# Node rows of a graph layer made by GpSimd, and one routing step moved in front of the first expert

## The chip, the core and the metric

One core of a Trainium2 chip runs the whole kernel. The metric is the device time of one execution, in microseconds (us), and the median of several executions is compared. The core has five engines with queues of their own: TensorE (PE; its weight loads are PEld), VectorE (DVE), ScalarE (ACT), GpSimd (POOL) and SyncE (SP, which here only issues DMAs).

## The reference

A graph attention layer is followed by a mixture of experts. There are 3750 nodes of 256 features, 120,000 edges sorted by destination and 8 relations with 4 heads:

```
h = segment_sum(ex * feat_src) / segment_sum(ex)       # per destination node and head
x = x + h + bias                                       # the "node rows"
xn = layernorm(x);  logits = xn @ Wr + br
two best of 8 experts per node; weights from the softmax of their two logits
x = x + sum over the two experts of  w_e * (gelu(layernorm(xn) * g_e + b_e) @ W1_e + b1_e) @ W2_e + b2_e)
```

## The kernel before

The nodes lie in 30 tiles of 128 rows. Three stages follow each other, and each is a block that all engines enter and leave together.

**Node stage.** It computes the features of each node for each relation and stores them in DRAM. Its GpSimd adds the bias to x (L392).

**Edge stage** (`edge_stage`). It runs over 32 groups of edge blocks. GpSimd gathers features (L798). VectorE scales them (L905) and adds sums from PSUM into `acc` (L914). TensorE multiplies by one-hot matrices (L1154). `acc` holds, per node, 256 weighted sums and 4 denominators. The last group is written out by hand in `last_period` of the vector block. There the first tile of the group is first rescaled (`carry_over`, L919 and L921), and then the sums are added pair by pair. Four PSUM banks hold the sums, so the matmul of a pair waits until VectorE has added the pair four before it. GpSimd has issued its last gather at 1806.6 us and then idles to the end of the stage.

**Route and expert stage** (`route_expert_stage`). It works in three batches of node tiles, 0 to 5, 6 to 15 and 16 to 29 (`BATCHES_R`). Most work goes by pairs of tiles. For a batch:

- `inverse` makes 1/denominator (L1768, L1769).
- `mean_pair` multiplies `acc` by it (L1750), and `node_pair` adds the mean to the node rows `xs` (L1754). `xs` lies in a buffer of `gath` and was loaded near the end of the edge stage. In batch 2 ScalarE makes the means (L1686) and VectorE only the sums.
- TensorE turns each pair (L1524) and multiplies by the router's weights (`pair_logits`, L1538); ScalarE copies the turned pair between the two (L1656).
- `statistics` (L1774) and `moments` (L166 to L171, L1782, L1783) make mean and variance. ScalarE takes the root (`deviation`, L1652). `factors` (L1789, L1790) makes scale and offset, and ScalarE writes the normalised rows (L1663).
- `choose` (L1799 to L1816) finds the two best experts. `counts` on TensorE (L1545 to L1547) counts rows per expert. `weigh` on ScalarE makes the weights (L1670). `place` (L1824 to L1840) turns all this into slots.
- GpSimd scatters each tile twice into `slots_x` in DRAM (L1482), in the order of the tiles.
- `hand_out` gives the expert steps their expert and their first row. Then `table_ready` lets SP load weights and rows.

An expert step n is `turn(n)` (L1556), `affine(n)` on VectorE (L1888), `first_layer(n)` (L1571), `gelu(n)` on ScalarE (L1680), `second_layer(n)` (L1587), `results(n)` on VectorE (L1901, L1904) and `add(n)`, an indirect DMA by GpSimd that adds to `out` (L1496). There are 43 steps. The order of all this on each engine is written out by hand. SP loads rows 0 and 1 when batch 0 is scattered. `ADDS_AFTER` says behind which tile's scatter GpSimd issues an `add`. The row loads from step 5 on wait for the scatters of batch 1.

The order in question on VectorE is: inverse, nodes, statistics and moments of batch 0, choose(0), inverse of all other tiles, place(0), nodes(1), hand_out, statistics and moments of batch 1, the node sums of batch 2, five of its statistics, then keep_tail(0), affine(0), choose(1), keep_tail(1), affine(1), place(1).

Of the kernel before, what the change touches and what calls it, by code (L numbers as in the profile page):

```python
# [24 lines left out]
ALU = mybir.AluOpType  # L25
# [3 lines left out]
P = 128  # L29
N_NODES = 3750  # L30
N_EDGES = 120000
D = 256
HEADS = 4
# [591 lines left out]
def edge_stage(nc, sb, edges, feats, xb, wr, br):  # L625
# [6 lines left out]
    with ExitStack() as ctx:  # L632
# [133 lines left out]
        with nc.Block() as block:  # L766
# [19 lines left out]
            @block.gpsimd  # L786
            def _(pool):
                def gather_features(g, r, n):
                    if not there(g):
                        return  # L790
                    if not isinstance(g, int) or g >= AHEAD:
                        wait_apart(pool, idx_ready, g - (AHEAD - 1), carrier)
                    for j in range(quads(g)):
                        if not isinstance(g, int) or g >= GBUFS:

                            wait_apart(pool, sum_ready, freed(g, j), carrier)
                        for u in range(j * QUAD, (j + 1) * QUAD):
                            pool.indirect_dma_start(gath[:, r, u], None, feats,  # L798
                                                    bass.IndirectOffsetOnAxis(ap=idxT[:, r, u:u + 1], axis=0)).then_inc(gath_in[r], 16)

                each_period(pool, gather_features, GBUFS + 1, GROUPS - 2)

            @block.vector
            def _(dve):
# [131 lines left out]
                def last_period(g, r, ra):  # L936
# [16 lines left out]
                    add(a, 7, ra, sums7)  # L953
                    carry_over(g, sums0[0])
# [285 lines left out]

def step_index(n):

    if n < FIRST3:
        return n
    at = HALVES_OF[FIRST3:n].count(HALVES_OF[n])
    return FIRST3 + (at if HALVES_OF[n] == 2 else N_BIG + at)

def route_expert_stage(nc, sb, experts1, experts2, b2, slots_x, out):
# [6 lines left out]
    with ExitStack() as ctx:  # L1256
# [18 lines left out]
        rden = t("rden", [P, TILES, HEADS])  # L1275
# [111 lines left out]

        def batch_of(n):
            return [n < hi for _, hi in BATCHES_R].index(True)
# [12 lines left out]
        with nc.Block() as block:  # L1402
            @block.sync
            def _(sp):
# [19 lines left out]
                def store(b):  # L1424
                    sp.wait_ge(xs_ready, BATCHES_R[b][1] // 2)
                    sp.dma_start(out_tiles[:, batch(b)], xs[:, batch(b)]).then_inc(out_stored[b], 16)
# [10 lines left out]
                sp.wait_ge(xs_ready, BATCHES_R[1][1] // 2)  # L1437
# [35 lines left out]
            def _(pool):  # L1473
# [31 lines left out]
                ADDS_AFTER = {10: [0], 13: [1], 15: [2], 18: [3], 22: [4]}  # L1505
# [10 lines left out]
            def _(pe):  # L1516
                def turn_pair(p):
                    pe.wait_ge(xs_ready, p + 1)
# [97 lines left out]
                turn_pair(first)  # L1616
                turn(0)
                first_layer(0)
                turn(1)
                counts(1)  # L1620
# [27 lines left out]
            def _(act):  # L1648
# [66 lines left out]
                copy_pair(first)  # L1715
                gelu(0)
                weigh(1)
# [22 lines left out]
            def _(dve):  # L1740
# [15 lines left out]
                def nodes(b):  # L1756

                    lo, hi = BATCHES_R[b][0] // 2, BATCHES_R[b][1] // 2
                    dve.wait_ge(x_in[b], 16)
                    mean_pair(lo)  # L1760
                    for p in range(lo, hi):
                        if p + 1 < hi:
                            mean_pair(p + 1)
                        dve.wait_ge(mean_done, p + 1)
                        node_pair(p)

# [4 lines left out]
                def statistics(b, of):  # L1771
                    dve.wait_ge(xs_ready, BATCHES_R[b][1] // 2)
# [134 lines left out]
                inverse(batch(0))  # L1907
                nodes(0)
# [67 lines left out]
def build(nc, ins, out):  # L1976
# [3 lines left out]
    with ExitStack() as ctx:  # L1980
# [22 lines left out]
        sb["small_in"] = ctx.enter_context(nc.semaphore("small_in"))  # L2003
        sb["x_in"] = [ctx.enter_context(nc.semaphore(f"x_in_r{b}")) for b in range(len(BATCHES_R))]
# [50 lines left out]
```

## Time and profile before

| | |
|---|---|
| median of 3 runs | 2462.4 us (2460.36 to 2465.61) |
| span of the profiled execution (first to last instruction) | 2456.4 us |
| mean granted TensorE clock | 0.813 |
| edge stage ends, route stage starts | 1883.4 us |
| first expert's first matmul | 1931.3 us |
| PE busy in 2100 to 2456 us | 345.2 of 356 us |
| weights of one expert step (w1, w2, b2), by the DMA issues | 1030 + 1024 + 128 KB |

The profile has no time for its execution beside the span; the median of the runs is 6.0 us above it, which is what lies before the first and behind the last instruction. A span is read stage by stage: TensorE is busy 77% of it as a whole, and nearly all of the last part.

### The profile page before, as it was taken

What the parts mean: (1) busy time and instruction counts of PE and PEld (TensorE: products, weight loads), DVE (VectorE), ACT (ScalarE), POOL (GpSimd) and SP (SyncE); (2) the same over time, 40 slices, a digit from 0 to 9 for tenths busy, and PEclk for the clock granted to TensorE, in tenths of its full rate; (3) what the DMA queues carried; (4) which work ended last, traced back from release to release, by engine and by line L of the source; (5) the groups of instructions that cost most, each with busy time, mean ns of one, the idle gap of its engine ahead of it and who ended that gap; (6) DMA issues with size and microseconds to landing.
All of it is one profiled execution on the core that took longest, in us unless ns stands there. A gap on an engine that the chain in (4) does not pass through costs nothing. (4 is left out here: it accounts for less than half of the span.)

```text
span 2456.4 us, 35279 instructions
## 1 busy us (share of the span) xinstructions
PE 1898.8 (77%) x9138; PEld 1594.8 (65%) x9139; DVE 1062.3 (43%) x3018; ACT 1076.9 (44%) x3259; POOL 1142.0 (46%) x1164
## 2 busy tenths in 40 slices
PE   8999125767767777867777777677877689999998
PEld 7887124656655665656565666565665668999887
DVE  6332013545555555545555555455567532221111
ACT  2222123645555545554555555454656532222221
POOL 4000744556666566666666566656620443122222
PEclk9999556787877768777787777777788689999999
DMA  6443422333333333333333333333312877777774
GB/s 239 189 170 143 109 67 74 84 90 88 90 92 92 88 88 91 90 88 90 88 92 92 89 90 90 92 85 88 91 44 80 282 230 221 248 246 247 241 234 104
DMA packets 121157, 315.51 MB, mean 128 GB/s; under 512 B 27047, under 2 KB 71335, under 8 KB 106180
## 3 DMA queue, kind: packets, MB, share of 16 engines
q0 software_dynamic: 60192, 149.24, 23.4%
q1 hardware_dynamic: 60836, 164.88, 19.3%
q8 instruction: 41, 0.67, 0.1%
q14 instruction: 88, 0.72, 0.1%
HBM read 257.36 MB, written 57.71 MB: 128 GB/s over the span
## 5 line engine op out<-in xcount | busy, mean ns | idle before, releaser
L798 POOL DMA_INDIRECT gath<-feats,idxT x996 | 950.6, 954 | 799.1 <-issue 272.7
L1154 PE MATMUL psP<-gath,hot 128*128 128x260 f32 x1992 | 668.1, 493 | 28.6 <-DVE gath L905 15.1
L1154 PEld LDWEIGHTS psP<-gath,hot 128*128 128x128 f32 x1992 | 469.4, 247 | 123.5 <-issue 35.4
L1113 PE MATMUL psOT<-cst,hot 128*128 128x128 f32 x996 | 196.1, 331 | 346.0 <-ACT hotT L1045 231.9
L1045 ACT COPY hotT<-psOT 128x512 f32<-128x512 f32 x249 | 143.5, 576 | 628.6 <-remote 485.4
L1113 PEld LDWEIGHTS psOT<-cst,hot 128*128 128x128 f32 x996 | 139.7, 171 | 407.2 <-issue 309.0
L1138 PEld LDWEIGHTS psE<-er,hotT 128*128 128x128 f32 x1992 | 309.7, 235 | 48.6 <-issue 44.9
L914 DVE TENSOR_TENSOR acc<-acc,psP 128x260 f32 x498 | 211.0, 424 | 295.3 <-remote 127.9
L1138 PE MATMUL psE<-er,hotT 128*128 x1992 | 309.5, 305 | 31.1 <-issue 19.9
L1035 ACT ACTIVATE hot<-cst,ndlT 128x128 f32<-128x128 f32 x996 | 316.2, 391 | 4.7 <-PEq L325 4.7
L1680 ACT ACTIVATE acc<-psH,w1buf 128x256 f32<-128x256 f32 (+1 forms) x344 | 122.4, 423 | 346.7 <-PE psH L1571 304.3
L1063 ACT ACTIVATE gath<-gath 128x64 f32<-128x64 f32 x1040 | 261.0, 337 | 0.1
L1496 POOL DMA_INDIRECT out<-acc,node x66 | 103.3, 1565 | 335.0 <-DVE acc L1904 178.0
L1571 PE MATMUL psH<-acc,w1buf 128*128 128x256 f32 (+1 forms) x1376 | 241.9, 334 | 4.4 <-issue 2.4
L1587 PE MATMUL psY<-w2buf,acc 128*128 128x256 f32 x1056 | 240.9, 384 | 3.4 <-issue 3.3
L905 DVE TENSOR_TENSOR gath<-gath,psA 128x1024 f32<-128x1024 f32 x184 | 224.5, 1221 | 27.2 <-ACT gath L1075 19.9
L1571 PEld LDWEIGHTS psH<-acc,w1buf 128*128 128x128 f32 x1376 | 217.8, 194 | 24.8 <-DVE acc L1888 2.9
L585 PE MATMUL psF<-wext,xT 128*128 128x264 f32 x960 | 221.1, 388 | 1.1 <-ACT xT L536 1.1
L1587 PEld LDWEIGHTS psY<-w2buf,acc 128*128 128x128 f32 x1056 | 200.0, 193 | 32.4 <-issue 6.8
L585 PEld LDWEIGHTS psF<-wext,xT 128*128 128x128 f32 x960 | 180.7, 191 | 31.6 <-ACT xT L536 1.5
L1038 ACT ACTIVATE hot<-hot 128x512 f32<-128x512 f32 x249 | 156.8, 630 | 38.3 <-remote 25.9
L1888 DVE TENSOR_SCALAR acc<-psX,w1buf 128x256 f32<-128x256 f32 (+1 forms) x86 | 37.5, 478 | 214.8 <-PE psX L1556 186.1
(232 smaller groups left out, 1178.5 us busy)
## 6 DMA issues: line engine op xcount, KB each, us to landing
w1buf<-in_experts SPq DMA_DIRECT2D x43, 1030.0 KB
w2buf<-in_experts SPq DMA_DIRECT2D x43, 1024.0 KB
feats<-frow SPq DMA_DIRECT2D x29, 1040.0 KB, 3.9
gath<-feats,idxT POOLq DMA_INDIRECT x996
meta<-in_edges SPq DMA_DIRECT2D x464, 12.0 KB
acc<-slots_x SPq DMA_DIRECT2D x23, 258.0 KB
gath<-in_b SPq DMA_DIRECT2D x43, 128.0 KB
acc<-slots_x SPq DMA_DIRECT2D x20, 129.0 KB
```

The costliest lines, as they stand in the source:

```text
L585: ins = pe.matmul(psF[:, n % BUFS, j, 0:W], xT[:, i % LEAD, k], wext[:, k, 2 * pair + j], start=k == 0, stop=k == KD - 1)
L798: pool.indirect_dma_start(gath[:, r, u], None, feats, bass.IndirectOffsetOnAxis(ap=idxT[:, r, u:u + 1], axis=0)).then_inc(gath_in[r], 16)
L905: dve.tensor_tensor(feat, feat, alpha.unsqueeze(3).to_broadcast([P, QUAD, HEADS, HD]), ALU.mult).then_inc(scaled, 1)
L914: dve.tensor_tensor(into[b % PQ], into[b % PQ], psP[:, bank(g, b, r), 0:FW], ALU.add).then_inc(sum_used, 1)
L1035: ins = act.activation(hot[:, r, u], iota, ACT.Square, bias=ndlT[:, r, u:u + 1])
L1038: act.activation(hot[:, r, j * QUAD:(j + 1) * QUAD], hot[:, r, j * QUAD:(j + 1) * QUAD], ACT.Relu, bias=1.0, scale=-1.0).then_inc(hot_read ...
L1063: ins = act.activation(feat, feat, ACT.Copy, scale=gath[:, r, u, D + h:D + h + 1])
L1113: ins = pe.transpose(psOT[:, k * P:(k + 1) * P], hot[:, r, j * QUAD + k], ident)
L1138: ins = pe.matmul(psE[:, u * W % 512:u * W % 512 + W], hotT[:, j % 2, k * P:(k + 1) * P], tables[k // BLK], start=True, stop=True)
L1154: ins = pe.matmul(psP[:, bank(g, b, r), 0:FW], hot[:, r, u], gath[:, r, u], start=u % BLK == 0, stop=u % BLK == BLK - 1)
L1571: ins = pe.matmul(psH[:, bank(n, g), at * slots(n):(at + 1) * slots(n)], w1(n, k, m), xeT[:, n % 2, k, 0:slots(n)], start=k == 0, stop=k = ...
L1587: ins = pe.matmul(psY[:, y_bank(n, j), 0:D], hT[:, n % 2, m, j * P:(j + 1) * P], w2(n, m), start=m == 0, stop=m == KH - 1)
```

## The change

GpSimd makes the means and node rows of pairs 0 to 6 (tiles 0 to 13), pairs 0 to 2 still inside the edge stage and pairs 3 to 6 in the route stage. For this VectorE makes 1/denominator of tiles 0 to 15 inside `last_period`, between the last add of the group before and `carry_over`. VectorE keeps pair 7. A pair is two GpSimd instructions of 128 x 512 f32, a product and a sum, both read twice from SBUF.

In the route stage choose(1) and place(1) of VectorE go in front of keep_tail(0) and affine(0), counts(1) of TensorE in front of turn(0), and weigh(1) of ScalarE in front of gelu(0). GpSimd scatters batch 1 up to tile 13 without a break, and then does add(0), where it did add(0) behind tile 10. The adds 1, 2 and 3 go behind tile 15.

```diff
@@ edge stage, GpSimd
                 each_period(pool, gather_features, GBUFS + 1, GROUPS - 2)
+                pool.wait_ge(sb["rden_early"], 1)
+                nodes_by_pool(pool, sb, 0, BATCHES_R[0][1] // 2, sb["x_in"][0])
@@ edge stage, last_period of VectorE
                     add(a, 7, ra, sums7)
+                    early = slice(0, BATCHES_R[1][1])
+                    step(dve.tensor_scalar(sb["rden"][:, early], acc[:, early, D:FW], 1e-30, None, ALU.max))
+                    step(dve.reciprocal(sb["rden"][:, early], sb["rden"][:, early]))
+                    dve.sem_inc(sb["rden_early"], 1)
                     carry_over(g, sums0[0])
+def nodes_by_pool(pool, sb, lo, hi, x_in):
+    def mean_pair(p):
+        t = slice(2 * p, 2 * p + 2)
+        part = acc[:, t, 0:D].rearrange("p t (h d) -> p t h d", h=HEADS)
+        pool.tensor_tensor(part, part, rden[:, t].unsqueeze(3).to_broadcast([P, 2, HEADS, HD]), ALU.mult).then_inc(mean_pool, 1)
+    mean_pair(lo)
+    pool.wait_ge(x_in, 16)
+    for p in range(lo, hi):
+        t = slice(2 * p, 2 * p + 2)
+        if p + 1 < hi:
+            mean_pair(p + 1)
+        pool.wait_ge(mean_pool, p + 1)
+        pool.tensor_tensor(xs[:, t], xs[:, t], acc[:, t, 0:D], ALU.add).then_inc(xs_pool, 1)
@@ route stage, GpSimd
                 ins.then_inc(keep_ready, 1)
-                ADDS_AFTER = {10: [0], 13: [1], 15: [2], 18: [3], 22: [4]}
+                nodes_by_pool(pool, sb, BATCHES_R[1][0] // 2, BY_POOL, x_in[1])      # BY_POOL = 7
+                ADDS_AFTER = {13: [0], 15: [1, 2, 3], 22: [4]}
@@ route stage, TensorE
                 turn_pair(first)
+                counts(1)
                 turn(0)
                 first_layer(0)
                 turn(1)
-                counts(1)
@@ route stage, ScalarE
                 copy_pair(first)
+                weigh(1)
                 gelu(0)
-                weigh(1)
@@ route stage, VectorE
-                inverse(batch(0))
-                nodes(0)
                 dve.wait_ge(sums_ready, 1)
...
                 factors(0)
+                mean_pair(BY_POOL)
+                dve.wait_ge(x_in[1], 16)
+                dve.wait_ge(mean_done, 1)
+                node_pair(BY_POOL)
                 dve.wait_ge(keep_ready, 1)
                 choose(0)
-                inverse(slice(BATCHES_R[0][1], TILES))
+                inverse(slice(BATCHES_R[1][1], TILES))
                 dve.sem_inc(rden_ready, 1)
                 place(0)
-                nodes(1)
                 units_left()
...
                 statistics(2, range(0, 5))
+                choose(1)
+                place(1)
                 keep_tail(0)
                 affine(0)
-                choose(1)
                 keep_tail(1)
                 affine(1)
-                place(1)
```

Whoever waited for `xs_ready` (the transposes, the statistics, SP's stores) now waits for GpSimd's count `xs_pool` up to pair 6 and for VectorE's from pair 7 (`wait_nodes`, `wait_batch`).

## Rows read from the trace of the kernel before

**Rows 1.** The page: busy time by engine; chain that ended last, by engine.
```profile
PE 1898.8 (77%) x9138; PEld 1594.8 (65%) x9139; DVE 1062.3 (43%) x3018; ACT 1076.9 (44%) x3259; POOL 1142.0 (46%) x1164
PE 20%; issue 1%; DMA 1%; POOL 0%; DVE 0%; another core or an unknown queue 0%; ACT 0%; SPq 0%; DVEq 0%; POOLq 0%
```

**Rows 2.** Windows: length, busy us by engine (instructions), granted clock, DMA share, GB/s.
```profile
1900.00:1920.00 20.00, 11.47 (x52) 10.58 (x52) 18.52 (x58) 16.57 (x61) 13.53 (x12) 0.50 0.50 170
1920.00:1940.00 20.00, 11.99 (x73) 11.11 (x73) 9.83 (x40) 11.25 (x23) 0.00 (x0) 0.63 1.03 362
1940.00:1960.00 20.00, 13.63 (x85) 12.92 (x84) 9.81 (x46) 7.37 (x17) 13.36 (x14) 0.80 0.72 251
...
2100.00:2456.00 356.00, 345.20 (x1845) 309.52 (x1843) 68.53 (x218) 86.64 (x240) 77.97 (x50) 0.99 0.71 219
```

**Rows 3.** Chain of waits, 1880 to 1960 us: start, length, what.
```profile
1883.67 0.31 DVE rden L1769
...
1916.77 6.56 DMA slots_x<-gath,slot_i
...
1924.12 5.58 DMA acc<-slots_x
...
1931.26 5.58 PE psH L1571 x32
...
1944.49 10.01 another core or an unknown queue
```

**Rows 4.** Timeline of VectorE and TensorE, end of the edge stage: start, length, instruction.
```profile
1875.09 0.43 DVE L921 TENSOR_TENSOR acc<-acc,phi 128x256 f32 x1
1875.55 0.99 DVE L914 TENSOR_TENSOR acc<-acc,psP 128x260 f32 x2
...
1872.82 9.20 PE L1154 MATMUL psP<-gath,hot 128*128 128x260 f32 x40 [0.89 <-DVE gath L905]
```

**Rows 5.** Timeline of GpSimd and VectorE, node stage.
```profile
0.26 0.10 POOL L2048 MEMSET const-float32-1.0<- 128x1 f32 x1
32.37 2.78 POOL L392 TENSOR_TENSOR x_biased<-x_rows,bias_all 128x256 f32<-128x256 f32 x4 [25.05 <-DMA bias_all<-in_bias]
...
32.43 0.71 DVE L167 TENSOR_TENSOR std<-stats 128x10 f32<-128x10 f32 x1
...
34.53 0.65 DVE L170 TENSOR_TENSOR mean<-stats 128x10 f32<-128x10 f32 x1
```

**Rows 6.** Timeline of VectorE, start of the route stage.
```profile
1887.94 2.06 DVE L1774 BATCH_NORM_STATS2 stats_r<-gath 128x6 f32<-128x256 f32 x6
1890.03 0.17 DVE L166 TENSOR_TENSOR mean_r<-stats_r 128x6 f32<-128x6 f32 x1
...
1894.14 0.21 DVE L1799 TENSOR_TENSOR lg<-psY,scl 128x48 f32<-128x48 f32 x1 [1.54 <-PE psY L1538]
...
1898.30 0.75 DVE L1769 RECIPROCAL rden<-rden 128x96 f32<-128x96 f32 x1
...
1900.15 0.17 DVE L1836 CAST slot_i<-slot_f 128x12 int32<-128x12 f32 x1
...
1910.47 0.16 DVE L1873 TENSOR_SCALAR row_of<-row_f 1x5 int32<-1x5 f32 x1
```

**Rows 7.** Timeline of ScalarE, route stage.
```profile
1899.14 6.79 ACT L1686 ACTIVATE acc<-acc,rden 128x64 f32<-128x64 f32 x28 [0.65 <-DVEq L1926]
...
1915.84 0.22 ACT L1652 ACTIVATE std_r<-std_r 128x20 f32<-128x20 f32 x1
```

**Rows 8.** Timeline of GpSimd and TensorE, route stage.
```profile
1951.60 0.97 POOL L1482 DMA_INDIRECT slots_x<-gath,slot_i  x1 [0.30 <-issue]
1948.69 0.39 PE L1571 MATMUL psH<-acc,w1buf 128*128 128x128 f32 x2 [0.55 <-issue]
...
1955.16 1.88 PE L1538 MATMUL psY<-wr_even,xtT 128*128 128x8 f32 x8 [4.80 <-ACT xtT L1656]
...
1989.70 7.17 PE L1571 MATMUL psH<-acc,w1buf 128*128 128x256 f32 x32 [0.89 <-DVE acc L1888]
```

More of the change, by code:

```diff
@@ L953, in last_period @@
                     add(a, 7, ra, sums7)
+                    early = slice(0, BATCHES_R[1][1])
+                    assert BASES[LAST] - (EBLOCKS - 1) >= BATCHES_R[1][1]
+                    step(dve.tensor_scalar(sb["rden"][:, early], acc[:, early, D:FW], 1e-30, None, ALU.max))
+                    step(dve.reciprocal(sb["rden"][:, early], sb["rden"][:, early]))
+                    dve.sem_inc(sb["rden_early"], 1)
                     carry_over(g, sums0[0])
@@ L1238, in rows_of_nodes @@
     return words[:, 0:TILES * D].rearrange("p (t d) -> p t d", t=TILES)
+def nodes_by_pool(pool, sb, lo, hi, x_in):
+    acc, rden, xs, mean_pool, xs_pool = sb["acc"], sb["rden"], rows_of_nodes(sb), sb["mean_pool"], sb["xs_pool"]
+    def mean_pair(p):
[10 more added lines that the diff above has]
+        pool.tensor_tensor(xs[:, t], xs[:, t], acc[:, t, 0:D], ALU.add).then_inc(xs_pool, 1)
 def step_index(n):
@@ L1274, in route_expert_stage @@
         wr_even = t("wr_even", [P, KD, E])
-        rden = t("rden", [P, TILES, HEADS])
+        rden, xs_pool = sb["rden"], sb["xs_pool"]
         stats = t("stats_r", [P, BT, 6])
@@ L1386, in pair_bank, with wait_nodes, wait_batch @@
             return p % 2 if p < BATCHES_R[2][0] // 2 else 1
+        BY_POOL = BATCHES_R[1][1] // 2 - 1
+        def wait_nodes(eng, p):
+            if p < BY_POOL:
+                eng.wait_ge(xs_pool, p + 1)
+            else:
+                eng.wait_ge(xs_ready, p - BY_POOL + 1)
+        def wait_batch(eng, b):
+            hi = BATCHES_R[b][1] // 2
+            wait_nodes(eng, min(hi, BY_POOL) - 1)
+            if hi > BY_POOL:
+                wait_nodes(eng, hi - 1)
         def batch_of(n):
@@ L1424, in store @@
                 def store(b):
-                    sp.wait_ge(xs_ready, BATCHES_R[b][1] // 2)
+                    wait_batch(sp, b)
                     sp.dma_start(out_tiles[:, batch(b)], xs[:, batch(b)]).then_inc(out_stored[b], 16)
@@ L1436, in _ @@
                 load_weights(1)
-                sp.wait_ge(xs_ready, BATCHES_R[1][1] // 2)
+                wait_batch(sp, 1)
                 sp.wait_ge(scattered[0], 32 * SIZE[0])
@@ L1517, in turn_pair @@
                 def turn_pair(p):
-                    pe.wait_ge(xs_ready, p + 1)
+                    wait_nodes(pe, p)
                     free = p - 1 if p < BATCHES_R[2][0] // 2 else p
@@ L1754, in node_pair @@
                     dve.tensor_tensor(xs[:, t], xs[:, t], acc[:, t, 0:D], ALU.add).then_inc(xs_ready, 1)
[L1756 to L1765, printed above, removed]
                 def inverse(of):
@@ L1771, in statistics @@
                 def statistics(b, of):
-                    dve.wait_ge(xs_ready, BATCHES_R[b][1] // 2)
+                    wait_batch(dve, b)
                     for i in of:
@@ L2003, in build @@
         sb["small_in"] = ctx.enter_context(nc.semaphore("small_in"))
+        sb["rden"] = keep("rden", [P, TILES, HEADS])
+        sb["rden_early"], sb["xs_pool"] = ctx.enter_context(nc.semaphore("rden_early")), ctx.enter_context(nc.semaphore("xs_pool"))
+        sb["mean_pool"] = ctx.enter_context(nc.semaphore("mean_pool"))
         sb["x_in"] = [ctx.enter_context(nc.semaphore(f"x_in_r{b}")) for b in range(len(BATCHES_R))]
```

## The prediction

> **What bounds the kernel now.** I read the page first. TensorE is busy 77% of the span and no other engine reaches half; the chain that ended last is named TensorE for a fifth of the span and hardly anything else [rows 1]. The windows by stage say where that holds. In 2100 to 2456 us TensorE is busy 345 of 356 us at full clock, and a change here could not shorten it. In 1900 to 1940 us it is busy 23.5 of 40 us at a clock of 0.50 and 0.63 [rows 2]. So what the change can win or lose is the time at which the packed expert part begins, plus gaps up to about 1990 us. The third view, the chain of waits, gives the order of that stretch: inverse, nodes and statistics of batch 0 on VectorE, logits, choose(0), place(0), then 12 scatters, 6.56 us until the last has landed, 5.58 us to load rows 0, and first_layer(0) at 1931.26 [rows 3]. Slots of batch 0 are ready at 1900.3 [rows 6], call it S; first_layer(0) starts at S + 30.9.
>
> **What an instruction of GpSimd costs.** The trace has a sum of 128x256 with both inputs in SBUF: 4 in 2.78 us, 0.70 each. A memset of one element is 0.10 [rows 5]. For 128x512 the bounds are 0.70 (no price per element) and 1.40 (twice). With 0.1 fixed it is 1.3 and I take that. No row shows a product with a broadcast input; I give it the same.
>
> **What it does to VectorE.** Before the first of those four GpSimd instructions VectorE's small sums take 0.17 us [the same kind in rows 6]. While the four run, its instructions L167 to L170, also with two inputs in SBUF, take 0.71 to 0.65 us each [rows 5]: one goes through per GpSimd instruction and GpSimd is not slowed. So beside instructions of 1.3 us I price each such VectorE instruction at 1.3. The lower bound is its own length, 0.17.
> The Trainium skill (SBUF — State Buffer, Who interferes with whom) says this of the chip: a VectorE instruction with two SBUF inputs contends with a GpSimd instruction that reads SBUF, and the later one blocks until the other is done. The trace agrees, 0.71 instead of 0.17 us. By that rule work handed to GpSimd isn't beside VectorE's but in its way; without the rule the sum would be the first rival below.
>
> **Part 1, end of the edge stage.** Added to VectorE are one small scalar instruction (0.2) and a reciprocal of 64 columns; between 0.31 for 24 and 0.75 for 96 columns it is 0.55 [rows 3, 6]. With the waits that is 0.8 us in front of carry_over. GpSimd then starts its first product, and L921 (acc times phi, both in SBUF, normally at 1875.09) waits for its end, at 1875.7 + 1.3 = 1877.0. The adds of the group start at 1877.6, not 1875.55 [rows 4]. TensorE's 40 records take 9.2 us, 0.92 a pair; it runs two quads by 1876.5 and then needs the first pair added. From there VectorE's order (two adds, a scale, two adds, 1.0 + 1.2 + 1.0 us) paces it: pair 9 ends 6.5 us behind the first add, at 1884.1 instead of 1882.0. The stage ends 2.1 us later, at 1885.5. Bounds: 0.85 if L921 isn't held, 3.3 if L919 in front of it is held too. GpSimd's six instructions, 7.8 us and the 0.45 of L921, end at 1884.0 and are hidden; at 1.4 each they still are.
>
> **Part 2, to the slots of batch 0.** Times from the stage's start (T). VectorE loses inverse and nodes of batch 0, 0.5 + 3.6 us. It waits for the ones' product (0.95) and makes its six statistics (2.06) by 3.2; before it was 6.6. GpSimd starts its eight instructions at 0.6 and ends at 11.0. Moments has five instructions with two SBUF inputs (1.0 us before), each now one GpSimd instruction long: it ends at 10.5, not 4.9. Before it ended at 8.0. Constants and factors, 1.15, are done at 11.65; pair 7 on VectorE, 0.69 twice and a wait, at 13.1. The logits are no longer what choose(0) waits for: TensorE can turn pairs from 0.9 and needs about 7.6 us (1886.0 to 1894.0 before), 8.5. choose(0) 3.8, inverse of 14 tiles 0.8, place(0) 1.15 [rows 6]: slots at T + 18.9 = 1904.4, against 1900.3. S moves by +4.1.
>
> **Part 3, from the slots to first_layer(0).** nodes(1), 6 us, is gone between place(0) and hand_out, so the table is ready at S + 4.2 instead of S + 10.3 [rows 6], and SP's first two sets of weights, 4.4 MB, go out 6 us sooner. They no longer share the DMA (half busy in 1900 to 1920, full behind it [rows 2]) with the last scatters and with rows 0: 3 us less for each of the two [rows 3]. So rows 0 land at about S + 24 instead of S + 29.4. They are no longer last. ScalarE's 14 means and four copies take 15.4 us from rden_ready and end the root of batch 1 at R + 16.7 [rows 7], R being S - 1.2: S + 15.7 with its latency. VectorE must wait for it in factors(1) (0.5), then has four node sums (2.5) and five statistics (1.7), then choose(1), which had run behind affine(0) (17 instructions as in choose(0), each some 0.03 longer for 80 columns: 4.4): S + 24.9. TensorE's counts(1) is 0.9, turn(0) ends at S + 26.5. ScalarE's ten normalised tiles and one copy end at 24.7, a table load (1.28) and weigh(1) at 26.3. place(1) 1.1, keep_tail and affine(0) 1.0: first_layer(0) at S + 28.7. Against S + 30.9 that is -2.2. With S at +4.1 the first layer starts 1.9 us later, 1933.1.
>
> **Part 4, behind it.** Before, GpSimd issues ten scatters of batch 1, 0.97 and 0.30 each, the last at 1951.60, so from 1940.1 to 1952.6; then it waits for add(0). In this stretch ScalarE stands for 10 us, with a releaser that the profile doesn't know, until 1954.5 [rows 3], and TensorE, busy 13.6 of 20 us, goes on at 1955.16 [rows 2, 8], 2.6 us behind the last scatter. What holds it I can't tell; the run of scatters is the nearest thing in time. Now place(1) ends at S + 27.4, 16 scatters of 1.27 us start 0.9 behind it at 1932.7 and end at 1953.0. If the stall goes with their end, TensorE continues at 1955.6, +0.4 us. The lower bound is no stall, the upper one with more of TensorE's work behind it, both below. Scattering tiles 14 and 15 sooner takes away the late load of step 5, and with it 0.9 us of gap at 1989.7 [rows 8]. The moved adds cost nothing: GpSimd's share is 1.6 us each and results(2) needs add(0) only near 1980.
>
> **Sum.** +1.9 at the first layer, -1.5 until 1955, -0.9 at step 5: -0.5 us on a span of 2456.4. The runs' median is 6.0 above the span, so I predict 2462 us. A difference under 0.2%, 4.9 us, can't be told from none.
>
> **Rivals.**
> 1. *No interference, or a short GpSimd instruction.* L921 isn't held (stage end +0.85), moments ends at T + 4.9, pair 7 is done at 7.5 and the logits at 8.5 set choose(0): slots at T + 14.2 = 1898.5, S at -1.8, the first layer at -4.0, and with the -2.3 of part 4 the sum is -6.3: 2456. For it: nodes really leave VectorE, 10 us in all. Against: rows 5.
> 2. *The stall of 1944 to 1955 goes.* Weights are in earlier, DMA has less piled up. TensorE would not stand 6 us, nor run at half clock until about 1964 (4 us): 2452 to 2454. For it: a DMA share of 1.03 in 1920 to 1940. Against: it is 0.72 in 1940 to 1960, not full, and the stall is there [rows 2].
> 3. *The longer run of scatters starves the others* (slower). 16 instead of 10 without a break, starting with first_layer(0) and not 9 us into the experts. TensorE's matmuls break up at 1948.1, 8 us into the run of before [rows 8]. At 1932.7 + 8 = 1940.7 it would have done 7.4 us less of its work than at 1948.1 before, and resume at the same 1955.6: +7 us, 2469. It decides if any engine's supply ends within the first 12 us of the run. Against: beside the 12 scatters from 1901 on ScalarE makes its means without a gap [rows 7].
> 4. *The change does its part but L919 is held too and moments' scalar instructions as well*: +1.2 and +1.0 more, 2464; inside "same".
>
> **Chances.** Forecast, with rival 4, 0.42; rival 1 0.21; rival 2 0.16; rival 3 0.21. Faster by over 0.2%: most of rivals 1 and 2, and the forecast's lower tail, 0.36. Slower: rival 3 and an upper tail of 0.04, 0.25. Same 0.39. The forecast's own range is 2458 to 2466. To hold 8 in 10 it must reach rival 2 below and rival 3 above: 2451 to 2470.
>
> **What would show it.** GpSimd's 128x512 at 1.3 us; VectorE's L166 to L170 at 1.3 us each beside them, L921 held; the route stage starting near 1885.5; slots of batch 0 near 1904; the table 4 us behind them; factors(1) waiting for ScalarE; first_layer(0) near 1933; TensorE standing until some 2.6 us behind the sixteenth scatter; no gap in front of step 5. I am wrong if L166 to L170 stay at 0.17 us, or if the gaps of 1940 to 1960 change by more than 3 us.

## The result and the profile after

The kernel after takes 2470.2 us in the median of 14 runs, the kernel before 2460.5 in 14 runs of the same chip: ratio 1.0038, 95% interval [1.0026, 1.0051]. On a second chip, with 5 runs of the kernel after, it was 1.0063 [1.0045, 1.0080]. So the change costs 0.4 to 0.6%, 10 to 15 us, where I forecast no difference; the time lies 0.2 us above the upper end of my range (2470).

The page after, busy time by engine and the chain by engine. It answers to [rows 1], and looks the same: the loss is not to be seen there.
```profile
PE 1888.1 (76%) x9138; PEld 1585.3 (64%) x9139; DVE 1059.5 (43%) x3004; ACT 1077.4 (44%) x3260; POOL 1155.3 (47%) x1178
PE 20%; DVE 1%; issue 1%; ACT 1%; another core or an unknown queue 0%; POOL 0%; DVEq 0%; POOLq 0%
```
The windows after (columns as in [rows 2]; the last is moved by 10 us).
```profile
1900.00:1920.00 20.00, 7.63 (x36) 7.13 (x36) 17.02 (x74) 16.50 (x51) 8.09 (x9) 0.50 0.21 58
1920.00:1940.00 20.00, 9.29 (x42) 8.39 (x42) 9.33 (x26) 14.42 (x33) 5.43 (x6) 0.50 0.86 312
1940.00:1960.00 20.00, 12.72 (x78) 11.44 (x78) 8.55 (x37) 5.30 (x12) 11.63 (x12) 0.77 0.95 310
1960.00:1980.00 20.00, 14.69 (x70) 12.96 (x70) 5.67 (x30) 7.15 (x17) 8.12 (x8) 0.66 0.42 147
...
2110.00:2466.00 356.00, 348.98 (x1874) 313.15 (x1872) 69.75 (x220) 88.91 (x248) 79.10 (x51) 0.99 0.73 222
```
From 1900 to 1960 TensorE is busy 29.6 us, 7.5 less than the 37.1 of [rows 2]; from 2110 on it is as full as before. So the loss arises ahead of the packed experts, where I had looked for any change. The profiled spans differ by 13.6 us (2470.0 and 2456.4), the medians by 9.7. The profiled run after took 1.8 us more than its span, and all other runs that have both figures on record 1.8 to 1.9; the 6.0 us that I added to the span of before is thus for the most part a profiled execution that was faster than the median. By marks in the two timelines (one profiled run each) the 13.6 us are:

| stretch | before | after | difference |
|---|---|---|---|
| VectorE's last sum of the edge stage ends | 1882.9 | 1886.9 | +4.0, of which 2.35 were there ahead of the first changed instruction |
| from there to the route stage's start (T) | 0.5 | 5.4 | +4.9 |
| T to the slots of batch 0 (S) | 16.9 | 18.7 | +1.8 |
| S to first_layer(0) | 30.9 | 34.1 | +3.1 |
| first_layer(0) to step 5 (first 128x256 layer) | 58.4 | 60.1 | +1.7 |
| step 5 to the end | 466.7 | 464.8 | -1.9 |

**The start of the route stage.** VectorE and GpSimd at the end of the edge stage after (start, length, instruction; it answers to [rows 4]).
```profile
1877.42 0.55 DVE L959 RECIPROCAL rden<-rden 128x64 f32<-128x64 f32 x1
1878.24 0.94 DVE L921 TENSOR_TENSOR acc<-acc,phi 128x4 f32 x1 [0.26 <-DVE rden L959]
1879.10 0.41 DVE L923 TENSOR_TENSOR acc<-acc,phi 128x256 f32 x1
...
1885.90 0.99 DVE L916 TENSOR_TENSOR acc<-acc,psP 128x260 f32 x2 [0.53 <-DVE acc L916]
```
```profile
1878.12 2.29 POOL L1255 TENSOR_TENSOR acc<-acc,rden 128x512 f32<-128x512 f32 x2 [68.32 <-DVEq L960]
...
1882.61 2.50 POOL L1264 TENSOR_TENSOR gath<-gath,acc 128x512 f32<-128x512 f32 x2
1892.30 0.20 POOL L1540 MEMSET ones_r<- 128x128 f32 x1 [7.19 <-POOLq L766]
```
VectorE is done at 1886.9 and GpSimd at 1885.1; without the 2.35 us that were there before, both are about where I put them. But the next stage's first instruction comes at 1892.30, and what it waited for is GpSimd's own queue at L766, the line that opens the edge block. The sequencer instructions of that line say what is there (duration in ns, first and last start in us), first before, then after.
```profile
L766 POOLq DRAIN  x1: 10786/10786/10786, 1803.7 to 1803.7; - x1
```
```profile
L766 POOLq DRAIN  x1: 9362/9362/9362, 1882.7 to 1882.7; - x1
```
**The route stage.** VectorE after, its small sums and the slots ([rows 6]).
```profile
1899.43 1.20 DVE L170 TENSOR_TENSOR mean_r<-stats_r 128x6 f32<-128x6 f32 x1
1900.66 1.19 DVE L171 TENSOR_SCALAR mean_r<-mean_r 128x6 f32<-128x6 f32 x1
1901.89 0.17 DVE L1813 TENSOR_SCALAR std_r<-std_r 128x6 f32<-128x6 f32 x1
...
1910.82 0.17 DVE L1867 CAST slot_i<-slot_f 128x12 int32<-128x12 f32 x1
```
```profile
1914.82 0.16 DVE L1904 TENSOR_SCALAR row_of<-row_f 1x5 int32<-1x5 f32 x1
```
L167 to L171 take 1.0 to 1.2 us each beside GpSimd's instructions of 1.04 and 1.26, and the ones behind them 0.17 when these are over; the table is there 4 us behind the slots. ScalarE after, then VectorE ([rows 7]):
```profile
1921.03 0.56 ACT L1698 COPY xtT<-psX 128x512 f32<-128x512 f32 x1
1921.49 2.02 ACT L1728 ACTIVATE acc<-acc,rden 128x64 f32<-128x64 f32 x8
1928.99 0.58 ACT L1698 COPY xtT<-psX 128x512 f32<-128x512 f32 x1 [5.48 <-remote]
...
1931.85 0.22 ACT L1694 ACTIVATE std_r<-std_r 128x20 f32<-128x20 f32 x1
```
```profile
1932.10 0.28 DVE L1820 RECIPROCAL scl<-std_r 128x20 f32<-128x20 f32 x1 [9.87 <-ACT std_r L1694]
```
The fourth copy comes 5.48 us late and the root 20.9 us behind the slots instead of 15.5. VectorE no longer has the nodes of batch 1 to make in this stretch; it has done their statistics and three sums of batch 2 by 1922.2 and then stands 9.87 us for the root. The chain of waits after ([rows 3]) has this stall, the first layer and the next stalls on it:
```profile
1923.51 5.45 another core or an unknown queue
...
1945.06 5.73 PE psH L1613 x32
1951.00 3.03 issue
1954.03 3.84 PE psH L1613 x32
```
ScalarE and TensorE behind that, answering to [rows 8]:
```profile
1953.20 1.14 ACT L1722 ACTIVATE acc<-psH,w1buf 128x128 f32<-128x128 f32 x4 [3.18 <-remote]
1967.31 2.17 ACT L1722 ACTIVATE acc<-psH,w1buf 128x128 f32<-128x128 f32 x8 [12.97 <-remote]
```
```profile
1964.44 0.59 PE L1629 MATMUL psY<-w2buf,acc 128*128 128x256 f32 x1 [1.72 <-issue]
1965.83 0.58 PE L1629 MATMUL psY<-w2buf,acc 128*128 128x256 f32 x1 [0.80 <-issue]
1967.23 4.43 PE L1629 MATMUL psY<-w2buf,acc 128*128 128x256 f32 x10 [0.82 <-issue]
```
TensorE's matmuls stand apart until 1967.2, 2.4 us behind the sixteenth scatter (it ends at 1964.84); no gap stands in front of step 5 any more.

**What the fourth copy waits for.** The profile's views name no releaser ("remote"), but the trace also records when each semaphore was raised. As a rule that is 0.01 us behind the end of the instruction that raises it. The fourth copy waits for TensorE's turned pair. By the (modelled) ends of the matmuls that pair is ready at 1922.14; its increment is recorded at 1928.97, and the copy starts at 1928.99. It is the same in other runs:

| kernel | matmuls end | increment recorded | copy starts |
|---|---|---|---|
| after | 1922.14 | 1928.97 | 1928.99 |
| nodes_only | 1933.31 | 1940.37 | 1940.39 |
| order_only (fifth copy) | 1925.77 | 1931.26 | 1931.28 |
| before (the long stall of [rows 3]) | 1946.68 | 1954.50 | 1954.53 |

ScalarE's own increments come late in the same stretch of the kernel after: two are recorded at 1924.60 and 1928.13, while the last mean that could have raised them ended at 1923.51, by a measured and not a modelled end. So ScalarE stands for a semaphore that is raised 5 to 8 us late while GpSimd issues scatters one behind the other.

### The profile page after: what moved, and what is told of

Read it like the earlier page. It is cut to its first block and busy times, and to the rows that moved or that the text cites. A ratio compares the mean times of both kernels' runs of the same rounds, so it can differ in the third digit from the quotient of the medians.

```text
span 2470.0 us, 35286 instructions
## 1 busy us (share of the span) xinstructions
PE 1888.1 (76%) x9138; PEld 1585.3 (64%) x9139; DVE 1059.5 (43%) x3004; ACT 1077.4 (44%) x3260; POOL 1155.3 (47%) x1178
## 5 line engine op out<-in xcount | busy, mean ns | idle before, releaser
L1161 PE MATMUL psP<-gath,hot 128*128 128x260 f32 x1992 | 653.4, 484 | 28.6 <-DVE gath L907 14.9
L1161 PEld LDWEIGHTS psP<-gath,hot 128*128 128x128 f32 x1992 | 459.1, 242 | 119.7 <-issue 34.9
L907 DVE TENSOR_TENSOR gath<-gath,psA 128x1024 f32<-128x1024 f32 x184 | 224.5, 1221 | 27.6 <-ACT gath L1082 20.1
L1045 ACT ACTIVATE hot<-hot 128x512 f32<-128x512 f32 x249 | 156.9, 630 | 41.1 <-remote 29.6
```

The lines of the kernel that those rows point to most:

```text
L907: dve.tensor_tensor(feat, feat, alpha.unsqueeze(3).to_broadcast([P, QUAD, HEADS, HD]), ALU.mult).then_inc(scaled, 1)
L1045: act.activation(hot[:, r, j * QUAD:(j + 1) * QUAD], hot[:, r, j * QUAD:(j + 1) * QUAD], ACT.Relu, bias=1.0, scale=-1.0).then_inc(hot_read ...
L1161: ins = pe.matmul(psP[:, bank(g, b, r), 0:FW], hot[:, r, u], gath[:, r, u], start=u % BLK == 0, stop=u % BLK == BLK - 1)
```

## The experiments

All were timed in five rounds beside the kernel before on the same chip, 11 or 12 runs each (after_again and half_ops 5); the medians of before differ by up to 15 us between chips, so only ratios are compared across the groups. The marks are of one profiled run each: from VectorE's last sum to T, T to S, S to first_layer(0), and T to the end.

| kernel | to T | T-S | S-fl0 | T-end | ratio to before, 95% |
|---|---|---|---|---|---|
| before | 0.5 | 16.9 | 30.9 | 573.0 | 1 |
| after | 5.4 | 18.7 | 34.1 | 577.7 | 1.0038 [1.0026, 1.0051] |
| late_memset | 5.6 | 16.9 | 29.5 | 569.1 | 1.0021 [1.0007, 1.0036] |
| early_drain | 0.5 | 18.5 | 34.2 | 576.5 | 1.0021 [1.0005, 1.0036] |
| nodes_only | 5.4 | 18.7 | 27.1 | 570.7 | 1.0022 [1.0006, 1.0038] |
| order_only | 0.5 | 16.9 | 31.4 | 572.0 | 0.9996 [0.9984, 1.0007] |
| after_again | 5.4 | 18.7 | 34.2 | 576.7 | 1.0063 [1.0045, 1.0080] |
| half_ops | 6.7 | 18.8 | 34.3 | 577.0 | 1.0064 [1.0047, 1.0081] |
| paced | 5.4 | 18.7 | 28.7 | 575.7 | 1.0034 [1.0019, 1.0049] |
| table_first | 0.5 | 16.9 | 27.6 | 567.8 | 0.9993 [0.9976, 1.0009] |
| pool_in_route_only | 0.5 | 21.8 | 34.2 | 579.0 | 1.0026 [1.0007, 1.0046] |
| drain_breaks | 0.5 | 18.5 | 28.6 | 573.2 | 1.0008 [0.9992, 1.0024] |
| before_breaks | 0.5 | 16.9 | 31.9 | 571.4 | 0.9998 [0.9980, 1.0016] |
| before_all | 0.5 | 16.9 | 27.9 | 566.2 | 0.9983 [0.9967, 1.0000] |
| nodes_drain | 0.5 | 18.5 | 27.1 | 571.7 | 0.9994 [0.9980, 1.0007] |
| table_again | 0.5 | 16.9 | 27.5 | 571.9 | 0.9979 [0.9964, 0.9994] |
| table_breaks | 0.5 | 16.9 | 28.1 | 566.9 | 0.9986 [0.9969, 1.0004] |

T-end of kernels that are alike from T on differs by 4 us (before and late_memset; table_first and table_again), so single differences below that are not read.

**late_memset: does a late instruction of GpSimd delay the stage by itself?** The kernel before; GpSimd waits for the last sum but one and clears one element.
```diff
                 each_period(pool, gather_features, GBUFS + 1, GROUPS - 2)
+                pool.wait_ge(sum_ready, sum(SIZES) - 1)
+                pool.memset(late[:], 0.0)
```

> The kernel before, with one addition: in the edge stage GpSimd waits for the last but one sum of the last group and then clears one element per partition. It moves no other work. Theory A (closing drain): GpSimd's queue ends each stage with a DRAIN that lasts about 7 us beyond its last instruction where the stage has issued indirect DMAs (1807.6 to 1814.5 us before the change, hidden by 69 us of idling; 1885.1 to 1892.1 after it). Then the memset at about 1881.5 is followed by some 7 us, the route stage starts near 1888.6 instead of 1883.4, and the kernel is 4 to 5 us slower. Theory B (the loss comes from VectorE and GpSimd holding each other, and from the order of the route stage): no change, within 1 us.

Its GpSimd, then VectorE, whose last sum ended at 1895.29:
```profile
1893.61 0.10 POOL L804 MEMSET late<- 128x1 f32 x1 [73.04 <-PE psP L1157]
1900.88 0.20 POOL L1502 MEMSET ones_r<- 128x128 f32 x1 [7.17 <-POOLq L767]
```
```profile
1900.92 0.19 DVE L1771 TENSOR_SCALAR rden<-acc 128x24 f32<-128x24 f32 x1 [5.63 <-PEq L767]
```
0.1 us of work holds the stage for 5.1 us, and the kernel is 0.2% slower. The node work isn't needed for it. The node stage, which issues no indirect DMA on GpSimd, has the reverse in the kernel before: its drain there ends at 58.0, 0.07 us behind GpSimd's last sum.
```profile
L325 POOLq DRAIN  x1: 8291/8291/8291, 49.7 to 49.7; - x1
```

**early_drain: can the drain be paid earlier?** The kernel after, with a drain of GpSimd's queue right behind its last gather.
```diff
+                pool.drain()
                 pool.wait_ge(sb["rden_early"], 1)
                 nodes_by_pool(pool, sb, 0, BATCHES_R[0][1] // 2, sb["x_in"][0])
```

> The changed kernel with one addition: a drain of GpSimd's own queue directly behind its last gather, 60 us before it gets its new work. Theory A, in the form that the time belongs to the indirect DMAs issued and is paid once: the closing drain shrinks to below 1 us, the route stage starts about 5 us earlier, 2465 us. Theory A, in the form that each drain costs it anew: the same 7 us, 2470 us. Theory B: 2470 us.

Its explicit drain and the one that closes the block:
```profile
L802 POOLq DRAIN  x1: 11554/11554/11554, 1816.8 to 1816.8; - x1
```
```profile
L766 POOLq DRAIN  x1: 2485/2485/2485, 1893.2 to 1893.2; - x1
```
The long one now lies in 67 us of idle time. The closing one ends 0.07 us behind GpSimd's last instruction, and the stage starts 0.5 us behind VectorE's last sum. 1.0021 remains.

**nodes_only and order_only: the two halves alone.** nodes_only is the kernel after with the second batch's choice, counts, places and the adds back in their old places; order_only is the kernel before with the new ones:
```diff
-                ADDS_AFTER = {10: [0], 13: [1], 15: [2], 18: [3], 22: [4]}
+                ADDS_AFTER = {13: [0], 15: [1, 2, 3], 22: [4]}
... (counts(1) in front of turn(0), weigh(1) in front of gelu(0))
+                choose(1)
+                place(1)
                 keep_tail(0)
                 affine(0)
-                choose(1)
                 keep_tail(1)
                 affine(1)
-                place(1)
```

> The changed kernel with the route stage's order of before (choose, counts, weigh and place of the second batch behind the first expert steps, adds where they were): only the work handed to GpSimd is left of the change. Theory A: it carries the whole loss of stage end and VectorE's wait, so 8 to 10 us slower than before. Rival C (the new order and the 16 scatters in one run are the loss): near 2461 us, within 2 us of before.

> The kernel before with only the second part of the change: choose(1), place(1), counts(1) and weigh(1) in front of the first expert step, and the adds behind tiles 13 and 15. Theory A: within 3 us of before. Rival C: 5 to 10 us slower, with TensorE standing during the run of scatters that starts beside the first expert step.

The nodes alone bring first_layer(0) 3.8 us closer to the slots, and still lose 0.2%. The order alone costs nothing measurable. ScalarE's stall at the fourth copy is 5.7 us in nodes_only, where nothing on the path waits for the root, and 0.67 us in order_only. There the fifth copy, behind the root, stands another 2.85 us, as it stands 3.40 in before:
```profile
1919.46 0.59 ACT L1656 COPY xtT<-psX 128x512 f32<-128x512 f32 x1 [3.40 <-remote]
```
Only together do the halves put a stall of 5.5 us on the path.

The scatters themselves differ between the two groups. Where VectorE makes the nodes of batch 1, three of the twelve are stretched and lie 1.8 us apart; where GpSimd has made them, all twelve are 1.27 apart. In before, beside nodes(1), then in after:
```profile
1904.79 1.49 POOL L1482 DMA_INDIRECT slots_x<-gath,slot_i  x1 [0.30 <-issue]
1906.58 0.97 POOL L1482 DMA_INDIRECT slots_x<-gath,slot_i  x1 [0.30 <-issue]
```
```profile
1914.52 0.97 POOL L1523 DMA_INDIRECT slots_x<-gath,slot_i  x1 [0.30 <-issue]
```
The longer the unbroken end of that run, the longer ScalarE stands at the fourth and fifth copy together: 5.5 to 5.7 us with twelve (after, nodes_only, after_again, nodes_drain), 3.4 to 3.5 with nine (before, late_memset, order_only), none with six (table_first and table_again, where the stretched ones come later). No run changes this alone.

**after_again, half_ops, paced.** after_again is the kernel after once more. half_ops gives GpSimd each tile by itself (128x256). paced puts two breaks of some 3 us into the scatters, one behind tile 3 (batch 0) and one behind tile 9 (batch 1):
```diff
                 for n in range(TILES):
                     scatter(n)
+                    if n in (3, 9):
+                        for k in range(8):
+                            pool.memset(pause[:], 0.0).then_inc(paused, 1)
+                            pool.wait_ge(paused, (n == 9) * 8 + k + 1)
```

> The changed kernel once more, unaltered, as the mark for the runs beside it on the same chip: 0.3 to 0.45% slower than before. The route stage starts some 5 us after VectorE's last add; slots of batch 0 18.7 us behind the start of the stage (18.69), first_layer(0) 34 us behind the slots.

> The changed kernel with GpSimd's means and sums one tile at a time (128x256), twice as many instructions of half the length. Theory H (VectorE's instructions with two SBUF inputs each wait for the GpSimd instruction under way): VectorE's L167 to L171 take about 0.6 us instead of 1.0 to 1.2, the slots of batch 0 are ready 2 to 2.5 us sooner behind the start of the stage (16.5 instead of 18.7), L921 of the edge stage is held half as long, and the kernel is 2 to 3 us faster than the changed one. Rival (the two engines share something that costs the same in total): L167 to L171 still at 1 us, no gain.

> The changed kernel with two breaks of about 3 us (eight small memsets in a chain) in GpSimd's scatters, behind tile 3 and behind tile 9; all scatters and DMAs stay. Theory R (ScalarE, VectorE and TensorE stand because GpSimd issues indirect DMAs without a break, and go on 2 us behind the end of the run): ScalarE's stall before the fourth copy, 5.5 us up to 2 us behind the twelfth scatter, goes or ends with the first break, so first_layer(0) starts 3 to 5 us sooner behind the slots (30 instead of 34 us); the stall of 1951 to 1967 is cut in two and TensorE runs between. The kernel is 2 to 6 us faster than the changed one although its scatters end 3 us later. Rival L (load on the DMA engines holds them): the stalls last as long as before or end with the loads; no gain or 3 us slower.

half_ops by lines and forms (last columns: busy us, mean ns, idle before), GpSimd and VectorE in its route stage:
```profile
L1265 POOL TENSOR_TENSOR gath<-gath,acc 128x256 f32<-128x256 f32 x14 | 9.7, 722 | 0.0
L1255 POOL TENSOR_TENSOR acc<-acc,rden 128x256 f32<-128x256 f32 x14 | 8.4, 629 | 68.4 <-DVEq L960 68.4
```
```profile
L167 DVE TENSOR_TENSOR std_r<-stats_r 128x6 f32<-128x6 f32 x1 | 0.6, 648 | 0.0
L171 DVE TENSOR_SCALAR mean_r<-mean_r 128x6 f32<-128x6 f32 x1 | 0.5, 539 | 0.0
L1815 DVE TENSOR_SCALAR std_r<-std_r 128x6 f32<-128x6 f32 x1 | 0.5, 533 | 0.0
```
Each VectorE instruction is held half as long (0.53 to 0.65 us instead of 0.96 to 1.20), but more of them are held, L166, L1815 and L1816 too, and the slots come no sooner (T + 18.8). Against VectorE's last sum GpSimd's part in the edge stage ends 1.3 us later, and the stage starts 6.7 us behind VectorE's last sum instead of 5.4. The break in batch 0 takes the stall away and brings first_layer(0) 5.5 us closer. Step 5 gains 0.6 us of it in the profiled runs (T + 110.2 instead of 110.8), since other stalls follow (8.4 us of ScalarE, up to 1972). The medians gain 3 us (2484.1 of 12 runs, 2487.2 of 5), and the two intervals overlap; so what the stall is worth at the end of the kernel is open.

**table_first: does the table need GpSimd?** The kernel before with the table handed out ahead of nodes(1).
```diff
                 place(0)
-                nodes(1)
                 units_left()
                 hand_out(units, 0, EARLY1, 1)
                 dve.sem_inc(table_ready, 1)
+                nodes(1)
```

> The kernel before with one move: VectorE hands out the first expert steps and releases the table before the node rows of batch 1 and not behind them, 6 us sooner. Nothing goes to GpSimd. Theory T (what the change won was only the early table): rows 0 land 3 to 5 us sooner and first_layer(0) starts 27 to 28 us behind the slots of batch 0 instead of 30.9, so 2 to 4 us faster than before. Rival (the run of scatters sets when TensorE goes on near 1955): first_layer(0) is sooner but the expert part continues at the same time, no change.

first_layer(0) comes 27.6 us behind the slots: for this mark one moved line gives what the nodes on GpSimd gave in nodes_only (27.1).

**pool_in_route_only, drain_breaks.** The first leaves pairs 0 to 2 to VectorE in the route stage and GpSimd its pairs 3 to 6; the second is early_drain and paced in one.

> The kernel after, but GpSimd makes no nodes in the edge stage: pairs 0 to 2 go back to VectorE at the head of the route stage, GpSimd keeps pairs 3 to 6 there; the new order stays. Theory (closing drain): GpSimd's last gather is then again 11 us ahead of VectorE's last sum, the drain runs beside the sums, and the route stage starts 0.5 us after VectorE's last sum instead of 5.4. Slots of batch 0 19 to 21 us after the stage's start (VectorE has six more instructions of 0.69 us, held by GpSimd's eight). ScalarE's stall of 5.5 us stays (GpSimd's scatters are as before) and first_layer(0) comes 34 us after the slots. Ratio to the kernel before 1.001 to 1.004. Rival: the late start belongs to GpSimd's node work as such; then it stays at 5 us and the ratio is 1.005 or more.

> The kernel after with both named costs taken out together: GpSimd drains its queue behind the last gather (stage start 0.5 us after VectorE's last sum), and takes two breaks of some 3 us in the scatters of batch 0 (behind tiles 3 and 9). Theory: the first gives back 4.9 us, the second brings first_layer(0) from 34 to 28.7 us after the slots, but as with the breaks alone 5 of those 5.5 us are lost again by step 5, since the scatters only come later and the next long run holds the rest. Then the ratio to the kernel before is 1.001 to 1.003. Rival (the two costs are all there is to the loss): 0.999 to 1.000.

In pool_in_route_only the stage starts 0.5 us behind the last sum, so the late start belongs to the place of GpSimd's last instruction, not to its node work; but the slots take 3.1 us more than in the kernel after, so the pairs made in the edge stage were worth that much. Here VectorE's products and sums of 128x512 stand against GpSimd's, and both are slowed: GpSimd's take 1.49 and 1.71 us instead of 1.04 and 1.26.
```profile
1907.07 1.71 POOL L1262 TENSOR_TENSOR gath<-gath,acc 128x512 f32<-128x512 f32 x1
```
drain_breaks has both named costs out, and 1.0008 cannot be told from no change. ScalarE in it, same stretch of work as above, without the stall:
```profile
1929.17 2.03 ACT L1734 ACTIVATE acc<-acc,rden 128x64 f32<-128x64 f32 x8
1931.22 0.59 ACT L1704 COPY xtT<-psX 128x512 f32<-128x512 f32 x1
```

**before_breaks, before_all.** The first has the breaks in the kernel before. The second adds to them the table first and a drain ahead of GpSimd's last `add`, which is two scatters:
```diff
                 for n in range(FIRST2, N):
+                    if n == N - 1:
+                        pool.drain()
                     add(n)
```

> The kernel before with the two breaks in the scatters of batch 0 and nothing else. Theory (a stall ends with the uninterrupted run of scatters in which it falls, and work held back is only moved): ScalarE's stall at the fifth copy goes or is under 1 us, first_layer(0) at most 1 us earlier since that stall was not on its path, the stall of 1944 to 1955 comes elsewhere; ratio 0.999 to 1.001. Rival (the stalls are pure loss and breaks shorten them): 0.997.

> The candidate for a version that beats both: the kernel before with the table handed out ahead of nodes(1) (first_layer(0) 27.6 us after the slots instead of 30.9, as run alone), the two breaks in the scatters of batch 0, and GpSimd's queue drained ahead of its last scatter of the expert stage, so that its closing drain, which ends 6.3 us after that scatter and with it the kernel, ends with it within 2.5 us. If the drain at the end is worth what the trace of before shows, the end comes 2 to 4 us earlier; with what the other two give, ratio 0.997 to 0.999. Rival (the drain only waits for the last write, wherever it stands; the gains ahead are given back in the expert stage): 1.000.

The breaks alone change nothing measurable, though the fifth copy's stall of 3.4 us is gone. The late drain wins nothing: the queue's drain is no cheaper there. GpSimd at the end of before_all, and the drain:
```profile
2454.01 1.55 POOL L1497 DMA_INDIRECT out<-acc,node  x1 [1.80 <-DVE acc L1911]
2463.45 1.56 POOL L1497 DMA_INDIRECT out<-acc,node  x1 [7.88 <-issue]
2465.32 1.55 POOL L1497 DMA_INDIRECT out<-acc,node  x1 [0.30 <-issue]
```
```profile
L1517 POOLq DRAIN  x1: 8819/8819/8819, 2453.8 to 2453.8; - x1
```
It ends 7.09 us behind the scatter in front of it and holds back the last two, about as much as it saves behind them: the closing drain ends 2.6 us behind the last scatter there and 6.2 in before.

**nodes_drain, table_again, table_breaks.** nodes_drain is nodes_only with the early drain; table_again is table_first once more; table_breaks adds the two breaks to it.

> The kernel after with the second batch's choice, counts and places and the adds back in their old places, and GpSimd's queue drained right behind its last gather. Only the nodes on GpSimd are left of the change, without the exposed drain. Theory (the drain is the nodes' whole loss): route stage 0.5 us after VectorE's last sum, slots of batch 0 at 18.5 us after it, first_layer(0) at 27.1 after the slots (as with the nodes alone); from the stage's start to the kernel's end some 571 us; ratio to the kernel before 0.999 to 1.001. Rival (the nodes on GpSimd cost more than the drain): 1.0015 to 1.0025 as with the drain exposed.

> The kernel before with the first batch's table handed out ahead of the second batch's nodes, once more. The first time first_layer(0) came 27.6 us after the slots (30.9 before), the stage's start to the end of the kernel was 567.8 us (573.0 before), and the ratio was 0.9993 [0.9976, 1.0009]. If the 3 to 5 us of the profile last, 0.998 to 0.999; if they are run variation (the same stretch was 569.1 with nothing changed in it), 0.9995 to 1.0005.

> The kernel before with the table ahead of the second batch's nodes and the two breaks in the scatters of batch 0, without the late drain. With that drain, which held the last two scatters back, the ratio was 0.9983 [0.9967, 1.0000]. Theory: the late drain was worth nothing or cost a little, so 0.998 again or below. Rival (the two together do no more than each alone): 0.9995 to 1.0005.

nodes_drain against nodes_only: 0.9994 [0.9980, 1.0007] instead of 1.0022 [1.0006, 1.0038], with the same marks but for T; the two were measured on different chips, each against before. The drain is the whole measurable loss of the nodes on GpSimd. The table ahead of nodes(1) was 0.9979 [0.9964, 0.9994] this time and 0.9993 the first; before_all and table_breaks, which contain it, had 0.9983 and 0.9986. That is 0.1 to 0.2% below before, at the edge of what can be measured: of the four intervals only that of table_again leaves out 1. Breaks add nothing to it.

## Why the prediction was wrong

*Part 1, "The stage ends 2.1 us later ... GpSimd's six instructions ... are hidden": this step failed.* The sum for VectorE was near (+1.65 from the first changed instruction on), and so was GpSimd's end. By luck in part: the instruction that I expected to be held, the 128x256 product (L921 before, L923 after), took 0.41 us for 0.43, and the 128x4 product in front of it (L919 before, L921 after), which I had held only in the upper bound and rival 4, took 0.94 for 0.16. What I left out is that a stage ends with the last drain and not with the last instruction. It costs 4.9 us net (late_memset 5.1 with no node work; gone in early_drain and pool_in_route_only). The trace of before had it, in the sequencers' instructions of the block's line: a drain of 10.8 us that ends 6.9 us behind the last gather. I priced what GpSimd executes and not its queue.

*Part 2, slots at T + 18.9:* 18.7. GpSimd's 128x512 took 1.04 us as a product and 1.26 as a sum, for 1.3 assumed of both; one VectorE instruction is held per GpSimd instruction, as the node stage of before showed. Five were held, as I had it, but not the same five: L166 still took 0.17 us, and the scalar instruction L171 was held (rival 4). That GpSimd is not slowed holds beside such small instructions; pool_in_route_only shows that it doesn't hold beside products and sums of 128x512. The Trainium skill (SBUF — State Buffer, Who interferes with whom) has it that a VectorE instruction with two SBUF inputs and a GpSimd instruction that reads SBUF block each other for a whole instruction. The trace agrees, and in half_ops the hold halves with the GpSimd instruction, 0.53 to 0.65 us.

*Part 3, first_layer(0) at S + 28.7: this step failed too.* It was 34.1. The table at S + 4.2 (4.0) and VectorE's wait for ScalarE's root were forecast; I took the root at S + 15.7, as if ScalarE's four copies ran without a gap, and it came at S + 20.9. Without the stall (paced, drain_breaks) the layer is at S + 28.6 to 28.7, my number. My argument against rival 3, that ScalarE makes its means without a gap beside the 12 scatters, was read from 1899 to 1906 only; ten us further on, the same timeline has the fifth copy standing for 3.4 us.

*Part 4:* the stall ends 2.4 us behind the sixteenth scatter (forecast 2.6), but that scatter ends at 1964.8, not 1953.0; the gap in front of step 5 is gone. From the first layer to step 5 it was 1.7 us more in this profile and 0.4 to 0.6 less in those of early_drain, after_again and half_ops, where I had 2.4 less: not told apart from noise.

*The rivals.* 3, the slower one, came out at the right time (2469), by luck: the stall that cost was ScalarE's, in the 12 scatters of batch 0, and a third to a half of the loss (4.9 us of 13.6 between the spans, 9.7 between the medians) was the drain, which no rival had. 1 and 2 did not occur: of the work handed to GpSimd no measurable part came back as time (nodes_drain 0.9994 [0.9980, 1.0007]), and ScalarE stands 13.0 us up to 1967.3 where it stood 10.0 up to 1954.5.

The two failed steps go with the loss: 1.0038 to 1.0063 with both, 1.0021 without the drain, 1.0008 without either. Each alone could not have been told well from noise, and these intervals overlap. The drain's share is shown, by four runs and by the marks. That the stall delays the first layer by 5.4 us is shown as well; how much of that reaches the end of the kernel is not (paced).

What stays open is why the semaphore is raised late. Breaks in the scatters take the stall away in both kernels that have the new order and the nodes on GpSimd, and the fifth copy's in before_breaks, so the scatters have part in it. In the kernel after it ends 2.0 us behind their run (1926.96), but the fourth copy's 0.67 us in order_only end inside the run, and behind the breaks ScalarE's stall up to 1972 ended inside one as well. table_again has no such stall beside its first 12 scatters, without a break but with three stretched ones. The Trainium skill (SBUF — State Buffer, Who interferes with whom) says that ScalarE never waits on another engine's ports, and the records above agree in that what it waits for is a semaphore. No run here shows what delays that, nor whether the stretched scatters alone make the difference between the nodes on VectorE and on GpSimd.

## What to carry to other kernels

Work handed to an idle engine late in a stage also moves that engine's closing drain: look at the sequencer's drain of the block's line before you call an engine's work hidden, and where its queue has issued indirect DMAs, let it drain while it is idle. When an order is tightened so that one engine waits for another, price the other by its worst gap in that stretch and not by its busy time. And before moving work to another engine to bring a result forward, try moving the result ahead of the work: for the first layer's distance from the slots one line did here what seven pairs on GpSimd did.

## What the runs showed of the hardware

- The drain of GpSimd's queue ends some 7 us behind the last instruction when many indirect DMAs were issued since the last drain, however long ago: 6.9 us behind the last gather (before), 7.0 (after, 75 us behind the last gather), 6.9 in late_memset, 7.1 in before_all; at the kernel's end, behind a wait for the last scatter, 6.2 (before). When none was, 0.07 us (early_drain's closing drain; the node stage). With only two since, at the end of before_all, it took 0.21 us and ended 2.6 behind the last scatter, so having issued any at all does not bring the 7 us.
- While GpSimd issues scatters one behind the other, semaphores of TensorE and ScalarE are raised up to 8 us late (TensorE's 1922.14 recorded at 1928.97 in after, 1946.68 at 1954.50 in before); the waiting ScalarE starts 0.02 to 0.03 us behind the record.
- VectorE's products and sums of 128x512 with two inputs in SBUF stretch GpSimd's scatters beside them from 0.97 to 1.49 us (before, order_only, table_again), and its products and sums from 1.04 and 1.26 to 1.49 and 1.71 (pool_in_route_only).
- An element-wise product with a broadcast input is faster on GpSimd than a sum of two full tiles, 1.04 and 1.26 us for 128x512, 0.63 and 0.72 for 128x256.
- Beside GpSimd, VectorE's scalar instructions of 6 columns are held as well (L171 1.19 us, L1815 in half_ops 0.53), not only those with two inputs.
